# Softmax denominators of a cross attention: columns of ones beside the values instead of sums on GpSimd

## The reference

```python
x = (hidden - mean) * rsqrt(var + 1e-5) * gamma + beta      # layer norm over 512
Q, K, V = heads(x @ Wq.T), heads(ctx), heads(ctx)           # 32 heads of 16
scores = einsum('bhsd,bhtd->bhst', Q, K) * 16 ** -0.5       # where(mask, ., -inf)
probs = softmax(scores, axis=-1)                            # over 1500 keys
attn = einsum('bhst,bhtd->bhsd', probs, V)
out = hidden + merge(attn) @ Wout.T
```

## Time and profile before

| | us |
|---|---|
| runs of the kernel, median of 3 | 1465.87 (1465.43 to 1465.91) |
| span of the profiled execution, first to last instruction | 1461.6 |
| TensorE matmuls busy | 1404.7 |
| VectorE busy | 1079.4 |
| ScalarE busy | 750.7 |
| GpSimd busy | 1243.8 |

### The profile page before, as it was taken

How to read it: one execution, slowest core, us unless ns; L and a number is a source line. 1 busy time by engine, 2 the same in 40 slices (tenths; PEclk the granted TensorE clock), 3 DMA queues, 4 the chain that set the end, 5 groups by cost and what they waited for, 6 DMA issues and landing times.

```text
span 1461.6 us, 66063 instructions
## 1 busy us (share of the span) xinstructions
PE 1404.7 (96%) x30000; PEld 992.2 (68%) x30000; DVE 1079.4 (74%) x3356; ACT 750.7 (51%) x623; POOL 1243.8 (85%) x434
## 2 busy tenths in 40 slices
PE   6999999999999999999999999999999999999986
PEld 4346667776777777766776776777777777766765
DVE  6657777777777777777787777777777777777730
ACT  2125555555555555555555555555555555555553
POOL 1009999999999999989999898999999999999996
PEclk8989999999999999999999999999999999999999
DMA  9303444444444344444544434354443444444320
GB/s 297 81 33 148 165 162 160 157 158 168 162 168 172 145 172 157 160 170 147 180 150 166 164 146 175 145 187 160 156 166 142 182 161 161 170 165 156 143 79 21
DMA packets 39161, 224.90 MB, mean 154 GB/s; under 512 B 4546, under 2 KB 4578, under 8 KB 26882
## 3 DMA queue, kind: packets, MB, share of 16 engines
q1 hardware_dynamic: 38882, 220.68, 41.5%
HBM read 216.90 MB, written 3.77 MB: 151 GB/s over the span
## 4 chain that ended last, share of the span: by engine, by line
PE 81%; DVE 10%; ACT 6%; issue 1%; DMA 1%; POOL 1%; ACTq 0%; SPq 0%; DVEq 0%; POOLq 0%
PE ps L237 23%; PE ps L292 19%; PE ps L277 17%; DVE masked L338 9%; PE ps L306 6%; PE ps L269 6%; ACT probs L373 6%; PE ps L254 4%; PE ps L670 4%; PE ps L245 1%; POOL sums L425 1%; DMA v<-in_wq_t 0%; DVE probs L578 0%; DVE den_inv L362 0%; PE ps L661 0%
## 5 line engine op out<-in xcount | busy, mean ns | idle before, releaser
L338 DVE CUSTOM_DVE_ANT_0 masked<-ps,mask_tile 112x500 bf16<-112x500 f32 x1536 | 980.0, 674 | 304.9 <-PE ps L237 286.0
L373 ACT ACTIVATE probs<-ps,mask_bias 125x1792 f32<-125x1792 f32 x384 | 673.9, 1755 | 616.6 <-PE ps L277 609.5
L425 POOL TENSOR_TENSOR sums<-sums,probs 125x1792 f32<-125x1792 f32 x191 | 763.1, 3995 | 14.6 <-ACT probs L373 5.7
L425 POOL TENSOR_TENSOR sums<-probs 125x1792 f32<-125x1792 f32 x96 | 383.7, 3997 | 179.5 <-ACT probs L373 177.9
L237 PE MATMUL ps<-kT,qdb 32*112 32x500 bf16 x1536 | 485.5, 413 | 19.6 <-DVE tile_max L338 15.7
L277 PEld LDWEIGHTS ps<-qd,kT 32*125 32x125 f32 x12288 | 423.7, 184 | 1.9 <-issue 0.9
L277 PE MATMUL ps<-qd,kT 32*125 32x112 f32 x12288 | 421.4, 268 | 0.8 <-issue 0.6
L292 PE MATMUL ps<-probs,v 125*32 125x112 f32 x12288 | 373.1, 261 | 2.1 <-issue 1.3
L292 PEld LDWEIGHTS ps<-probs,v 125*32 125x32 f32 x12288 | 298.8, 110 | 70.0 <-issue 46.2
L237 PEld LDWEIGHTS ps<-kT,qdb 32*112 32x112 bf16 x1536 | 161.3, 123 | 217.2 <-DVE tile_max L338 151.2
L269 PE MATMUL ps<-max_rows,ones_row 4*125 4x448 bf16 x1536 | 179.6, 392 | 14.3 <-ACT probs L373 11.1
(11 more groups left out here) (49 smaller groups left out, 256.2 us busy)
## 6 DMA issues: line engine op xcount, KB each, us to landing
kT<-in_kt SPq DMA_DIRECT2D x96, 1000.0 KB, 5.1
v<-in_ctx SPq DMA_DIRECT2D x96, 1000.0 KB
mask_tile<-mask_add SPq DMA_DIRECT2D x32, 328.1 KB, 13.7
x_res<-in_x SPq DMA_DIRECT2D x16, 224.0 KB, 14.3
out<-result SPq DMA_DIRECT2D x16, 224.0 KB, 13.9
probs<-in_x SPq DMA_DIRECT2D x14, 224.0 KB, 9.2
v<-in_wq_t SPq DMA_DIRECT2D x1, 1024.0 KB, 6.1
woutT<-in_wout_t SPq DMA_DIRECT2D x1, 1024.0 KB, 20.6
```

What stands on the lines that cost most here:

```text
L338: nc.vector.tensor_tensor_reduce(out=masked[0:PAIR_Q, t % 2, :], in0=bank[0:PAIR_Q, 0:KEYS], in1=mask_tile[0:PAIR_Q, b % 2, KEYS * c:KEYS ...
L373: nc.scalar.activation(probs[0:LANES, k % PROBS], ps[0:LANES, 0:TILES_R, 0:BANK_Q], ACT.Exp, bias=mask_bias[0:LANES, n:n + 1], scale=SCALE ...
L425: nc.gpsimd.tensor_tensor(total, before, probs[0:LANES, slot % PROBS], ALU.add).then_inc(summed, 1)
```

## The change

- Values come into a staging buffer of two chunks (`v_stage`). GpSimd copies each chunk from there into a wider `v` (`spread_values`), in which each pair has 48 columns: 16 of the first head, 16 ones, 16 of the second head. The ones are written once (`set_ones`).
- `times_values` makes one product for each head instead of one for each pair: 32 columns of `v` (the first head and the ones, or the ones and the second head) as weights, and that head's 56 columns of `probs`. So 32 products of 56 columns stand in a slot where 16 of 112 columns stood. Half of each output are the head's sums of values, the other half 16 copies of its denominator.
- `add_slot`, `add_denominators` and `last_denominators` are gone, and with them the waits of `exp_slot` for GpSimd.
- ScalarE copies bank 4 whole, once (`take_acc`). GpSimd picks the denominators' halves and the heads' halves by two products with masks and adds the two heads of each (`fold_heads`); VectorE exchanges the halves of 16 lanes in each 32 with a shuffle (`swap_denominators`, in slot 3) and inverts as before, now out of SBUF.
- Bank 5 joins the ring, which has three banks now; `masked` has three buffers. The transposed row maxima become a unit of the ring (`("rows", b)`, between tiles 2 and 3 of slot 10). VectorE copies them out (`take_rows`), and GpSimd spreads them in one instruction (`spread_rows`) in place of ScalarE.
- SP waits, ahead of each load of values, until the staging buffer's last chunk is copied (`v_ready`).

The core of the diff:

```diff
-GROUP = 4
-SUMS = SLOTS // GROUP
-ADDS = SUMS * (GROUP - 1)
+HEAD_GROUPS = 2 * BLOCKS
+PAIR_COLS = 3 * HEAD_DIM
+STAGES = 2
+RING_BANKS = [5, 6, 7]
+ACC_BANK = 4
+SWAP_AT = (3, 1)
...
         def load_v(sp, b, c):
+            n = CHUNKS * b + c
             src = ctx[b, KEYS * c:KEYS * (c + 1), :].rearrange("(m k) n -> m k n", k=CHUNK)
-            sp.dma_start(v[0:LANES, c], src).then_inc(v_landed[c], 16)
+            wait_over(sp, v_ready, n - STAGES + 1)
+            sp.dma_start(v_stage[0:LANES, n % STAGES], src).then_inc(v_landed[n % STAGES], 16)
...
         def times_values(pe, b, k):
             c = k // CHUNK
             if k % CHUNK == 0:
-                pe.wait_ge(v_landed[c], 16 * (b + 1))
+                pe.wait_ge(v_ready, CHUNKS * b + c + 1)
             if k == 0:
-                wait_over(pe, heads_taken, b)
-            for g in range(BLOCKS):
+                wait_over(pe, acc_taken, b)
+            for i in range(HEAD_GROUPS):
+                g, e = i // 2, i % 2
                 for r in range(TILES_R):
-                    col = 128 * g + ROW * r
-                    mm = nc.tensor.matmul(acc[ROW * r:ROW * (r + 1), g, :], v[0:LANES, c, k % CHUNK, col:col + ROW],
-                                          probs[0:LANES, k % PROBS, r, PAIR_Q * g:PAIR_Q * (g + 1)],
-                                          start=(k == 0 and g == 0), stop=(k == SLOTS - 1),
+                    mm = nc.tensor.matmul(acc[ROW * r:ROW * (r + 1), i, :],
+                                          v[0:LANES, c, k % CHUNK, TILES_R * g + r, HEAD_DIM * e:HEAD_DIM * e + ROW],
+                                          probs[0:LANES, k % PROBS, r, QUERIES * i:QUERIES * (i + 1)],
+                                          start=(k == 0 and i == 0), stop=(k == SLOTS - 1),
                                           skip_group_check=True, tile_position=(0, ROW * r))
             mm.then_inc(pv_done, 1)
...
         def exp_slot(act, b, k):
             n = SLOTS * b + k
             wait_over(act, pv_done, n - PROBS + 1)
-
-            if n >= PROBS:
-                act.wait_ge(summed, (GROUP - 1) * ((n - PROBS) // GROUP) + max((n - PROBS) % GROUP, 1))
             act.wait_ge(scored, n + 1)
...
+        def spread_values(pool, b, c):
+
+            n = CHUNKS * b + c
+            pool.wait_ge(v_landed[n % STAGES], 16 * (n // STAGES + 1))
+            wait_over(pool, pv_done, CHUNK * (n - CHUNKS + 1))
+            halves = v[0:LANES, c].rearrange("p k i (h d) -> p (k i) h d", d=HEAD_DIM)[:, :, 0:3:2, :]
+            staged = v_stage[0:LANES, n % STAGES].rearrange("p k (i h d) -> p (k i) h d", h=2, d=HEAD_DIM)
+            nc.gpsimd.tensor_copy(halves, staged).then_inc(v_ready, 1)
...
+        def fold_heads(pool, b):
+
+            pool.wait_ge(acc_taken, b + 1)
+            pick_half(picked_den, 1).then_inc(den_picked, 1)
+            pick_half(picked, 0).then_inc(head_picked, 1)
+            wait_over(pool, den_swapped, b)
+            pool.wait_ge(den_picked, b + 1)
+            nc.gpsimd.tensor_tensor(den_across[:], picked_den[:, :, 0], picked_den[:, :, 1], ALU.add).then_inc(den_added, 1)
...
             for b in range(BATCH):
-                for a in range(ADDS):
...
+                if b < end:
+                    make_qd(pool, b + 1)
+                spread_values(pool, b, 1)
+                if b > 0:
+                    fold_heads(pool, b - 1)
+                if b + 2 < BATCH:
+                    make_qdb(pool, b + 2)
+                if b > 0:
+                    divide_heads(pool, b - 1)
+                spread_values(pool, b, 2)
+                if b < end:
+                    spread_rows(pool, b + 1)
+                    spread_values(pool, b + 1, 0)
```

More of the change, by code:

```diff
@@ L59, in slot_others, with slot_rows, slot_units @@
             if slot == k and after % 2 == b % 2 and b >= after]
+def slot_rows(b, k):
+    return [("rows", b + 1)] if k == ROWS_SLOT and b + 1 < BATCH else []
+def slot_units(b, k):
+    tiles = slot_tiles(b, k)
+    return tiles[0:3] + slot_rows(b, k) + tiles[3:4] + slot_others(b, k)
 FIRST_TILES = [("tile", 0, t) for t in range(MAX_TILES)] + [("tile", 1, t) for t in range(AHEAD)]
-RING = FIRST_TILES[:]
-RING += [unit for b in range(BATCH) for k in range(SLOTS) for unit in slot_tiles(b, k) + slot_others(b, k)]
+RING = FIRST_TILES + [("rows", 0)]
+RING += [unit for b in range(BATCH) for k in range(SLOTS) for unit in slot_units(b, k)]
 LAST_OUTS = [("out", d, part) for d in range(BATCH // 2 - 2, BATCH // 2) for part in range(OUT_PARTS)]
@@ L95, in build @@
         max_rows = sb("max_rows", [128, 2, BLOCKS, PAIR_Q], BF16)
+        rows = sb("rows", [128, PAIR_Q])
+        raw = sb("raw", [128, BLOCKS, 2, QUERIES])
+        picked = sb("picked", [128, BLOCKS, 2, QUERIES])
+        picked_den = sb("picked_den", [128, BLOCKS, 2, QUERIES])
+        heads = sb("heads", [128, BLOCKS, QUERIES])
+        den_across = sb("den_across", [128, BLOCKS, QUERIES])
+        den = sb("den", [128, BLOCKS, QUERIES])
         den_inv = sb("den_inv", [128, BLOCKS, QUERIES])
-        own = sb("own", [128, 2, BLOCKS, QUERIES])
-        heads = sb("heads", [128, BLOCKS, QUERIES])
         attnT = sb("attnT", [128, 2, BLOCKS, PAIR_Q])
@@ L238, in score_tile, with turn_rows @@
                              start=True, stop=True).then_inc(ring_filled, 1)
[L240 to L246, removed]
+        def turn_rows(pe, unit):
+            bank = ring_bank(pe, unit)
+            pe.wait_ge(neg_ready, unit[1] + 1)
+            nc.tensor.matmul(bank[:, 0:PAIR_Q], neg_max[0:PAIR_Q].rearrange("p r n -> p (r n)"),
+                             ident[0:PAIR_Q, 0:PAIR_Q], start=True, stop=True).then_inc(ring_filled, 1)
         def project_out(pe, unit):
@@ L295, in times_values @@
                                           skip_group_check=True, tile_position=(0, ROW * r))
             mm.then_inc(pv_done, 1)
[L298 to L322, removed]
@@ L338, in take_tile @@
             nc.vector.tensor_tensor_reduce(
-                out=masked[0:PAIR_Q, t % 2, :], in0=bank[0:PAIR_Q, 0:KEYS],
+                out=sums, in0=bank[0:PAIR_Q, 0:KEYS],
                 in1=mask_tile[0:PAIR_Q, b % 2, KEYS * c:KEYS * (c + 1)], scale=1.0, scalar=LOWEST,
@@ L374, in exp_slot, with take_acc @@
                                  bias=mask_bias[0:LANES, n:n + 1], scale=SCALE).then_inc(exped, 1)
-        def take_heads(act, b):
+        def take_acc(act, b):
             act.wait_ge(pv_done, SLOTS * (b + 1))
[L379 to L393, removed]
+            wait_over(act, head_picked, b)
+            nc.scalar.copy(raw[:].rearrange("p g e q -> p (g e q)"), ps[:, ACC_BANK, 0:BANK_Q]).then_inc(acc_taken, 1)
         def spread_q(pool, dst, b):
@@ L428, in add_heads @@
             wait_over(pool, attn_ready, b)
-            pool.wait_ge(heads_taken, b + 1)
-            nc.gpsimd.tensor_tensor(heads[:], own[:, 0], own[:, 1], ALU.add).then_inc(heads_added, 1)
+            pool.wait_ge(head_picked, b + 1)
+            nc.gpsimd.tensor_tensor(heads[:], picked[:, :, 0], picked[:, :, 1], ALU.add).then_inc(heads_added, 1)
         def divide_heads(pool, b):
-            pool.wait_ge(den_taken, BLOCKS * (b + 1))
+            pool.wait_ge(den_inverted, BLOCKS * (b + 1))
@@ L595, in _ @@
             take_max(dve, 0)
-            for unit in FIRST_TILES[MAX_TILES:]:
+            for unit in FIRST_TILES[MAX_TILES:] + [("rows", 0)]:
                 take_unit(dve, unit)
@@ L609, in _ @@
                         take_unit(dve, unit)
+            swap_denominators(dve, end)
             for g in range(BLOCKS):
@@ L642, in _ @@
                     if k == 0 and b > 0:
-                        take_heads(act, b - 1)
-                    if k == ROWS_SLOT and b < end:
-                        spread_rows(act, b + 1)
-            take_heads(act, end)
+                        take_acc(act, b - 1)
+            take_acc(act, end)
         @block.tensor
@@ L678, in _ @@
             pe.wait_ge(consts, CONSTS)
-            turn_rows(pe, 0)
+            turn_rows(pe, ("rows", 0))
             pe.wait_ge(wout_landed, 16)
```

140 lines of the change are left out of this document (70 added, 70 removed).

## The result

| | us |
|---|---|
| runs after, median of 4 | 1534.51 (1531.8 to 1536.33) |
| runs before beside them, median of 4 | 1465.65 (1464.49 to 1465.91) |
| ratio after to before, 95% interval | 1.0472 (1.0457 to 1.0487) |
| span of the profiled execution after | 1534.6 |

The kernel is 4.7% slower; 1534 was predicted. Of the ten runs of the kernel before with light loads (further down) one took 1742.04 us at a mean granted clock of 0.64, and the ratios leave it out.

What follows compares the result with a forecast made beforehand. TensorE's instruction fetch was taken to bound the changed kernel: 31 batches of 44.2 us plus 38 make 1408.2, +66.5; with start and end the span is 1529, plus 4.3 gives 1534 us. Own range 1480 to 1590, overall 1426 to 1605.

Steps and rivals of the forecast that it cites:

- Loop: Exponential, row maxima and scores form a closed loop through the same four banks; a plain slot takes 3.23 us.
- Values burst: TensorE's values products in a slot: time goes with columns, so 0.78 us as before; 1.54 us kept as a rival.
- rival 2: A round of four products stays at 0.096 us, burst 1.54 us: 46.8 us a batch, 1612 us; chance 0.12.
- A batch of 40.6 us without loaded fetches: Batch time without other limits: 38.8 us for twelve slots plus the remaining excess of slots 3 and 9 and row transpose.
- rival 1: Instruction fetch stays hidden, also in the load windows: 40.6 to 40.8 us a batch, 1425 us; chance 0.21.
- third bank: Tile 2 of a slot starts without waiting for VectorE: at most 0.2 us in slots 3 and 9, nothing in plain slots.
- denominators: Denominator bursts leave TensorE: 0.39 us in slot 3, at most 0.38 and 0.20 in slots 10 and 11.
- the split: On TensorE, 16 values products a slot become 32 of 56 columns; the burst takes 0.78 us, as before.
- GpSimd's copy: GpSimd copies each values chunk of 2048 elements out of the stage: 2.3 us, 1.8 to 4.6, hidden.
- Ends: Start: rows spread on GpSimd, +0.1 us; end: two products, an add and a shuffle in series, +1 us.
- the 4.3 us: The median of the runs was taken to lie 4.3 us above the profiled span, giving 1534 from 1529.
- Instruction blocks decide: TensorE's 9.9 blocks of 256 instructions a batch outrun fetches (quiet 3.8 us, loaded 5.5): 44.2 us a batch, +2.2.

Runs made afterwards that it cites:

- light loads: Key and value loads cut to 16 elements a partition from batch 2 on: kernel before 1458.72 us, kernel after 1421.68 us.
- light kernel: Kernel after, with key and value loads cut to 16 elements a partition from batch 2 on: 1421.68 us.
- five f32 kernels with the change and three banks: Kernel after 1534.51 us; with key and value loads cut to 16 elements a partition 1421.68, in quarters 1457.17, finer 1477.73, in six 1 MB windows 1618.94.
- the same quarters tied to two counts: Kernel after, key quarters loaded after a slot's scores, value quarters after its values burst, mask in thirds: 1477.73 us; both quarters after each slot: 1457.17 us.
- the third, alone: Kernel before with each values product of 112 columns issued as two of 56, nothing else changed: 1597.15 us, ratio 1.0909.
- the kernel with the six windows: Kernel after with value loads moved to after slots 1, 5 and 9, so six 1 MB load windows a batch instead of three of 2 MB: 1618.94 us.

## Why the prediction was right

**Loop, 3.23 us a plain slot.** Held: 3.22.

**Values burst, 0.78 by columns against 1.54 by count.** Held: x64 in 0.99 us busy against x32 in 0.95, so rival 2 is out. The Trainium skill's floor of some 25 ns for a matmul of up to 64 columns ("TensorE: Matmul & The Clock Gate", Back-to-back issue gap) doesn't add up over four column groups: one behind the other, 64 of them would be 1.6 us, and the trace has 0.99.

**A batch of 40.6 us without loaded fetches.** Measured 40.61 with light loads, 1421.68 us in all (1425 for rival 1). The terms inside were less good: third bank 0.4 predicted, 31.5 / 32 = 0.98 measured, because I gave slot 3 0.2 where it has 0.47, and slot 10 nothing where it has 0.49; denominators 0.87 predicted (0.39 + 0.38 + 0.20 - 0.1), 0.98 measured; the split 0, measured 0.80, some of it stops behind mask, result and residual loads, which stayed. The errors cancelled.

**GpSimd's copy, 2.3 us (1.8 to 4.6), hidden.** Its group after the change (count | busy, mean ns | idle before):

```profile
L417 POOL COPY v<-v_stage 125x2048 f32<-125x2048 f32 x96 | 181.9, 1894 | 80.2 <-DMA v_stage<-in_ctx 80.2
```

1.89 us, near the lower end. GpSimd is busy 390 us instead of 1244, and TensorE waits for it once, 5.1 us at the end of the kernel, where the last denominators, sums and products stand in series.

**Ends.** The first exponential starts 0.7 us later (106.31; 0.1 predicted), and after the last one 16.4 us remain instead of 14.3 (+2.1; +1 predicted). The exponentials span 1411.8 us (1408.2 predicted), the whole 1534.6 (1529); the 4.3 us that I added for what lies around the span did not appear, the median and the profiled span agree within 0.1. So three small misses of 3.6, 1.7 and 4.3 us nearly cancel. The 4.3 us were never what lies around the first and the last instruction, as the section on the time before has it: every run of the record is 1.7 to 2.1 us above its own span, and the profiled execution before was simply some 2.5 us faster than the median.

**Instruction blocks decide.** Held, and it is the step that the table of light loads shows: 319 packets (320 predicted), stops inside bursts at block borders, 3.6 a batch where I had three, 44.4 us a batch where I had 44.2. Not all stand behind a full DMA: 56 stops with 60% of the time do (engines over 60% busy from the block's start to its successor's packet, own count), and most of the others have a lighter load ahead of them. The Trainium skill's "mostly hidden" ("Runtime: NRT & Kernel Launch", Instruction fetch mechanics) held for this kernel with 7.3 blocks a batch and fails with 9.9 or more, little with light loads (25 stops, 17 us) and much with whole ones.

**What was mis-sized.** The loss over 40.6 was 3.6 a batch in the forecast and is 3.8, but I had put all of it on waiting for blocks. A part is TensorE's clock, which the prediction did not price; the 44.2 is right to that extent by luck. How it divides is not settled. From rows: the 119 us of stops lose some 0.5 each to slack (TensorE otherwise waits 0.45 to 0.62 for ScalarE in a plain slot), 119 - 56 = 63 us; at half clock a slot takes 4.1 us (exponentials at 216.38 and 220.48) to 4.4 (tiles at 213.54 and 217.98) instead of 3.22, so the 130 us at half clock in the batches cost 28 to 36. With the light kernel's share taken off that makes 85 to 92 of the 113 us. A straight line through the five f32 kernels with the change and three banks gives about 0.5 us for each us of stop and as much for each at half clock, within some 3 us, but the two go up together there, and the line can't tell them apart.

The fetch was mis-sized as well, in ways that partly cancel. By the packets (own count, from a block's first instruction to 1.4 us after its successor's packet has ended) a fetch takes 3.2 us in the median with light loads, where I had 3.8: the one that I measured ran with DMA 31% busy. It takes 3.9 in the kernel after, and behind DMA engines over 60% busy 4.9, 2.5 times a batch, where I had three of 5.5.

## What to carry to other kernels

Count instructions, not only columns: a split that leaves the burst's time as it is can cost 9% once a block of 256 TensorE instructions takes about as long to run as to fetch (here 4.1 us against 3.2 in the quiet and 4.9 behind loads), and most of the price is paid behind large loads. Look for "issue" inside a burst and for the instruction queue's packets in the profile of before; if they are there, cut the loads into pieces of a quarter MB and spread them before adding instructions, and time more than one order: the same quarters tied to two counts gave 1477.73 us instead of 1457.17. Weigh each part of a change by itself: here two parts were worth 31 us each, and the third, alone, cost 131.

## What the runs showed of the hardware

- TensorE's clock fell to half for 3.4 to 10.2 us at stops in the middle of a stream, none of them longer than 3.36 us: 24 times and 130 us in the batches after, and 280 us in all in the kernel with the six windows. In the kernel before, with 9 short stops, it never did once the batches were under way.
- With values products in bf16, one matmul each instead of two, TensorE stayed at 1.2 GHz nearly throughout (clock 0.533 over the span), even when the profile shows it busy all the time (0.50 from 112 to 1900 us). Why is open.
- TensorE's instructions come by the DMA engines that the loads use: a fetch took 3.2 us with light loads and 4.9 behind engines over 60% busy (medians). Loads of 1 MB delayed it no less than loads of 2 MB; quarters of a MB cut the mean stop from 1.06 to 0.70 us.
- GpSimd copies 2048 elements a partition in 1.89 us, while its addition of 1792 takes 4.0.
